# Row sums on the token partitions, inverses spread by a product, and another order of the attention's work

## The reference

```
q, k, v = norm(x) @ Wq, ctx @ Wk, ctx @ Wv      # x (4, 256, 128), ctx (4, 1601, 96)
attn = softmax(q k^T / 8)                       # per head, over 1601 keys
x = x + (attn v) @ Wo + bo
f = norm(x);  p = softmax(f @ router_w + router_b);  w = the two best of p
x = x + gelu(f @ sw1 + sb1) @ sw2 + sb2 + sum_e w_e (gelu(f @ rw1_e + rb1_e) @ rw2_e + rb2_e)
```

## Time and profile before

| | us |
|---|---|
| median of 3 runs (481.19 to 483.22) | 482.54 |
| the profiled execution | 480.71 |
| its span, first to last instruction | 478.9 |
| PE busy | 429.6 (90%) |
| DVE busy | 289.2 (60%) |
| POOL busy | 269.9 (56%) |
| ACT busy | 234.6 (49%) |

### The profile page before, as it was taken

One profiled execution on the slowest core, in us unless ns is written; L12 is line 12 of the kernel. 1 busy time (PEld: TensorE's weight loads), 2 busy tenths in 40 slices (PEclk: granted clock), 3 DMA queues, 4 the chain that ended last, 5 costly groups with the idle time before them and its releaser, 6 DMA issues. The chain is left out here.

```text
span 478.9 us, 9185 instructions
## 1 busy us (share of the span) xinstructions
PE 429.6 (90%) x3462; PEld 321.0 (67%) x3462; DVE 289.2 (60%) x595; ACT 234.6 (49%) x367; POOL 269.9 (56%) x184
## 2 busy tenths in 40 slices
PE   8999978988998986988998959898998896999997
PEld 7667655756674855665876738585857574687896
DVE  4666665766724764676627664767356773768653
ACT  5645370624381704351763516152826071579873
POOL 6209872958570747555721749091805479067982
PEclk9979988999999997999999997999999998999999
DMA  7400000200000002000000011000000000320500
GB/s 236 96 1 2 1 2 1 53 1 2 1 0 1 2 1 52 2 1 0 2 1 1 2 55 47 1 2 1 0 1 2 0 3 1 97 81 1 177 23 23
DMA packets 17138, 11.73 MB, mean 24 GB/s; under 512 B 10188, under 2 KB 14136, under 8 KB 17096
## 3 DMA queue, kind: packets, MB, share of 16 engines
q1 hardware_dynamic: 17096, 11.15, 8.8%
HBM read 10.55 MB, written 0.56 MB: 23 GB/s over the span
## 5 line engine op out<-in xcount | busy, mean ns | idle before, releaser
L908 DVE TENSOR_REDUCE maxes<-ps 128x1 f32<-128x402 f32 x256 | 133.1, 569 | 85.8 <-PE ps L1094 85.4
L792 ACT ACTIVATE probs<-ps 128x1024 f32<-128x1024 f32 (+1 forms) x112 | 104.0, 962 | 156.4 <-PE ps L1153 155.1
L489 POOL TENSOR_TENSOR work<-work,probs 128x1024 f32<-128x1024 f32 x60 | 142.7, 2378 | 4.8 <-POOL work L487 0.2
L1169 PE MATMUL ps<-probs,v_sb 128*64 128x256 f32 (+1 forms) x832 | 101.7, 391 | 0.0
L487 POOL TENSOR_TENSOR work<-probs 128x1024 f32<-128x1024 f32 x15 | 35.9, 2393 | 114.7 <-issue 93.6
L1169 PEld LDWEIGHTS ps<-probs,v_sb 128*64 128x64 f32 (+1 forms) x832 | 56.8, 139 | 33.4 <-issue 10.5
L905 DVE TENSOR_TENSOR kq_lo<-ps,kq_hi 128x402 fp32r<-128x402 f32 (+2 forms) x80 | 41.8, 544 | 55.0 <-ACT kq_hi L753 54.0
L1094 PE MATMUL ps<-kq_hi 64*128 64x402 f32 x256 | 60.0, 413 | 8.0 <-DVE maxes L908 7.1
L1153 PE MATMUL ps<-kq_hi,kq_lo 64*128 64x256 f32 (+1 forms) x416 | 62.1, 291 | 0.0
L1153 PE MATMUL ps<-kq_lo,kq_hi 64*128 64x256 f32 (+1 forms) x416 | 62.0, 291 | 0.0
L1153 PE MATMUL ps<-kq_hi 64*128 64x256 f32 (+1 forms) x416 | 62.0, 291 | 0.0
(11 more groups left out here) (149 smaller groups left out, 629.7 us busy)
## 6 DMA issues: line engine op xcount, KB each, us to landing
v_sb<-weight_rows SPq DMA_DIRECT2D x12, 256.0 KB, 3.8
raw<-in_ctx_T_dram SPq DMA_DIRECT2D x3, 600.4 KB, 4.6
work<-in_L_ffn_rw_dram SPq DMA_DIRECT2D x1, 1024.0 KB, 7.0
shift_rows<-neg_row SPq DMA_DIRECT2D x64, 0.5 KB, 2.0
raw<-weight_rows SPq DMA_DIRECT2D x4, 256.0 KB, 3.6
raw<-in_ctx_T_dram SPq DMA_DIRECT2D x3, 150.8 KB, 2.6
x_sb<-in_x_dram SPq DMA_DIRECT2D x1, 384.0 KB, 4.8
wo_sb<-in_L_xattn_Wo_dram SPq DMA_DIRECT2D x1, 256.0 KB, 6.5
```

Of the source, the lines that this page charges most:

```text
L489: ops.tensor_tensor(acc, acc, pr, ALU.add).then_inc(summed, 1)
L792: nc.scalar.activation(dst, src, ACT.Exp, scale=SCALE).then_inc(probs_ready, 1)
L908: v.tensor_reduce(maxes[:, p % 2, i * T + t, blk:blk + 1], src[:, 0:BW], AX.X, ALU.max).then_inc(ring_taken, 1)
L1169: ins = mm(o_bank[DH * i:DH * (i + 1), :], v_sb[0:rows, c, h * DH:(h + 1) * DH], probs[0:rows, n % SLOTS, i, j * S:(j + 1) * S], start=(c ...
```

## The change

- The folded sums are now the stationary operand and a single column of ones the moving one: four products of a result of 128 tokens by 1 (head i, token tile t) put the row sums on the token partitions, 4 columns in all. DVE takes the reciprocal of 128x4 numbers, once. This is the item "sums".
- A new item "spread": four products of a broadcast column of reciprocals with the identity give 64 equal rows for each head and tile, the inverses spread over 128 partitions as before. ACT copies the 128x256 result to SBUF (`inverse`), and DVE multiplies o_bank by it in one instruction of 128x256.
- All 16 maxima of pair n+1 stand beside the scores of pair n: a couple ahead of unit 0 and one behind each unit. None stands among the values.
- The sums of pair n-1 come behind the scores of pair n, the spread behind the first two projections. The add stands ahead of the values in the list, which on DVE is ahead of the next maxima as before.
- y and roots stand ahead of the context's splits, and norm stands behind the third unit of scores of the pair after. roots no longer waits for the add of its pair.
- DVE and not POOL folds the sums of pair 0 too; the statistics of x (stats) stand ahead of the scores of pair 0; normal one pair earlier; POOL's part of the w2 split (w2_low) behind the values of pair 14.

The diff, cut to its core:

```diff
-AMONG_VALUES = ((0, 2), (3, 4), (5, 2))
-BEHIND_VALUES = 2
...
     for n, (b, p) in enumerate(order):
-        ahead = maxima[n + 1][before_scores:] if n + 1 < n_order else []
-        behind = 2 if n == 1 else 0
+        ahead = maxima[n + 1] if n + 1 < n_order else []
+        out += ahead[:2]
         for u in range(n_units):
             out.append(("scores", (b, p, u)))
-            if n and u in (behind, behind + 2):
-                out.append(("quotient", order[n - 1] + ((u - behind) // 2,)))
...
+            out += ahead[2 * u + 2:2 * u + 4]
+            if u == 2 and p == 2 and b:
+                out.append(("norm", b - 1))
+        if ahead:
+            out.append(("shift", order[n + 1]))
...
+        if n:
+            out.append(("sums", order[n - 1]))
+            projections = projections[:2] + [("spread", order[n - 1])] + projections[2:]
...
+        if b and p == 1:
+            out += [("ring", ("y", b - 1)), ("roots", b - 1)]
...
+        out.append(("add", (b, p)))
+        out += [("values", (b, p, u, j)) for u, unit in enumerate(key_units(chunks)) for j in range(len(unit))]
+        if n == n_order - 2:
+            out += [("w2_low", e) for e in range(experts)]
...
-    amid = {0: [("sums", last_pair), ("quotient", last_pair + (0,)), ("quotient", last_pair + (1,))], 2: [("ring", ("y", b))], 5: [("ring", ("xt", b))],
+    amid = {0: [("sums", last_pair)], 1: [("spread", last_pair)], 2: [("ring", ("y", b))], 5: [("ring", ("xt", b))],
...
-            return "dve" if pair and u == NU - 1 or pair == B * PAIRS - 1 else "pool"
+            return "dve" if u == NU - 1 or pair == B * PAIRS - 1 else "pool"
...
                 if kind == "roots":
-                    if w + 1 < B:
-                        added(w + 1, 1)
                     inverse_roots(slice(w * T, w * T + T), B + w + 1)
...
+                elif kind == "spread":
+                    pair = w[0] * PAIRS + w[1]
+                    act.wait_ge(spread_filled, pair + 1)
+                    if pair:
+                        act.wait_ge(sums_taken, pair)
+                    nc.scalar.copy(inverse[:], sums_bank).then_inc(inverse_ready, 1)
...
-            def quotient(b, p, i):
-
-                pair, q = b * PAIRS + p, slice(i * P, i * P + P)
-                dve.wait_ge(sums_filled, pair + 1)
-                v.reciprocal(rden[:, q], sums_bank[:, q]).then_inc(rden_ready, 1)
-                dve.wait_ge(rden_ready, 2 * pair + i + 1)
+            def quotient(b, p):
+
+                pair = b * PAIRS + p
+                dve.wait_ge(inverse_ready, pair + 1)
...
-                v.tensor_tensor(oT[:, b % 2, p, q], o_bank[:, q], rden[:, q], ALU.mult).then_inc(sums_taken, 1)
+                v.tensor_tensor(oT[:, b % 2, p, :], o_bank, inverse[:], ALU.mult).then_inc(sums_taken, 1)
...
+                if kind == "sums":
+                    dve.wait_ge(sums_filled, w[0] * PAIRS + w[1] + 1)
+                    v.reciprocal(rden[:].rearrange("p h t -> p (h t)"), sums_bank[:, 0:2 * T]).then_inc(rden_ready, 1)
...
                 pe.wait_ge(summed, (pair + 1) * (NU - 1))
-                for i in range(2):
-                    ins = mm(sums_bank[DH * i:DH * (i + 1), :], ones[:, :],
-                             psum_keys[:, pair % 2, i, 0:S], start=True, stop=True)
+                for j in range(2 * T):
+                    i, t = divmod(j, T)
+                    ins = mm(sums_bank[:, j:j + 1], psum_keys[:, pair % 2, i, t * P:(t + 1) * P], ones[:, 0:1],
+                             start=True, stop=True)
                 ins.then_inc(sums_filled, 1)
+
+            def spread_inverses(b, p):
+
+                pe.wait_ge(rden_ready, b * PAIRS + p + 1)
+                for t in range(T):
+                    for i in range(2):
+                        ins = mm(sums_bank[DH * i:DH * (i + 1), t * P:(t + 1) * P],
+                                 rden[:, i, t:t + 1].to_broadcast([P, DH]), idr, start=True, stop=True)
+                ins.then_inc(spread_filled, 1)
```

More of the change, by code:

```diff
@@ L67, in plan @@
         out += pair_of_maxima + v0[3 + i:4 + i]
-    out.append(("shift", order[0]))
+    out += [("shift", order[0])] + [("stats", t) for t in range(1, batches)]
     rest = v0[len(couples) - 1:]
@@ L72, in plan @@
         out += [x] + rest[2 + i:3 + i]
-    out += rest[2 + len(second):] + maxima[1][:before_scores]
+    out += rest[2 + len(second):]
     for n, (b, p) in enumerate(order):
-        ahead = maxima[n + 1][before_scores:] if n + 1 < n_order else []
-        behind = 2 if n == 1 else 0
+        ahead = maxima[n + 1] if n + 1 < n_order else []
+        out += ahead[:2]
         for u in range(n_units):
             out.append(("scores", (b, p, u)))
-            if n and u in (behind, behind + 2):
-                out.append(("quotient", order[n - 1] + ((u - behind) // 2,)))
[L82 to L88, removed]
+            out += ahead[2 * u + 2:2 * u + 4]
[3 more added lines that the diff above has]
+            out.append(("shift", order[n + 1]))
         vs = [("ring", ("v", b, c)) for c in range(chunks)] if p == 0 and b else []
         projections = keys(n + 2)
+        if n:
+            out.append(("sums", order[n - 1]))
+            projections = projections[:2] + [("spread", order[n - 1])] + projections[2:]
         if vs:
@@ L98, in plan @@
         if n == 0:
-            out += [("stats", t) for t in range(1, batches)]
+            out += [("normal", t) for t in range(1, batches)]
         if n == 1:
-            out += [("normal", t) for t in range(1, batches)] + [("ring", ("xn", 0)), ("ring", ("xn", 1))]
+            out += [("ring", ("xn", 0)), ("ring", ("xn", 1))]
+        if b and p == 1:
+            out += [("ring", ("y", b - 1)), ("roots", b - 1)]
         if p == 1 and b + 1 < batches:
@@ L288, in build @@
         ones = sb("ones", [P, DH])
-        rden = sb("rden", [P, S])
+        rden = sb("rden", [P, 2, T])
+        inverse = sb("inverse", [P, S])
         oT = work[:, 1, :].rearrange("p (a b c) -> p a b c", a=2, b=PAIRS)
@@ L1048, in _ @@
                     row_sums(*w)
+                if kind == "spread":
+                    spread_inverses(*w)
                 if kind == "ring":
```

10 lines of the change are left out of this document (5 added, 5 removed).

## The result

The changed kernel takes 425.4 us (425.1 to 425.6), the kernel before 481.9 in the same series: a ratio of 0.8825, with a 95% interval from 0.8795 to 0.8854. The profiled execution took 425.6, its span 423.8 of it, at a mean granted clock of 0.992 (before 0.968).

What follows compares the result with a forecast made beforehand. The prediction took PE, busy nine tenths of the span, as the bound. Its terms, 9.3 + 9.0 + 25 + 16.4 - 2.8 - 0.9 = 56 us, took 480.7 to 424.7; forecast 425, range 417 to 430.

Steps and rivals of the forecast that it cites:

- A plain pair: Middle pairs: pitch falls from 21.1 to 18.6 us, 2.5 a pair, 25 over ten pairs.
- Maxima beside the scores: All maxima fit beside the scores, 8.3 us from first couple to scores' end; no waiting for DVE booked.
- the bound of two units: Scores: a loop of PE filling and ACT emptying, 2.35 us for two units; two couples of maxima just fit in.
- The rival of the maxima's queue: DVE's queue of maxima sets the scores' pace: 1.1 us per pair over 15 pairs, 441 us; chance 0.15.
- Sums and spread: New products on PE in each pair: sums 0.9 us, spread 0.75 with changes of tile.
- The thin cover for the reciprocal: Before the spread, PE's sums and projections cover DVE's reciprocal with 0.2 us to spare; 0.1 booked.
- The slower rival: Each of the sixteen small steps waits for its own weight load, 0.44 us each: 510 us; chance 0.02.
- Start and pair 1: Pair 1 begins at 43.75 instead of 53.04, 9.3 us gained; pair 1 itself gains 9.0.
- The terms of pair 0: Pair 0, without sums: 8.3 + 2.7 + 0.2 + 5.83 = 17.0 us.
- Pairs 6 and 10: Stall at the third unit and low clock behind it go, 0.7 booked for norm: 16.4 us gained together.
- Pairs 14 and 15: No projections cover the chain: 19.2 and 17.5 us, together 36.7 against 33.9, 2.8 lost.
- Experts: The experts' sums and spread cost 0.9 us more.

Runs made afterwards that it cites:

- e1: The changed kernel with ten of each pair's maxima back among and behind the values, six in the scores, DVE's add behind them: 460.4 us, ratio 0.9575.
- e3: The changed kernel with the old product of ones and 256-column reciprocal at the new place, no spread, no copy by ACT: 412.8 us, ratio 0.8592.
- e7: The changed kernel with every reduction of maxima over 201 of its 402 columns: 422.5 us, ratio 0.8783.
- e2: The changed kernel with the old sums back behind their own pair's values, DVE's reciprocals and products in the next scores: 424.6 us, ratio 0.8834.
- e6: The changed kernel with the four products of the sums done twice over, in one piece of sixteen steps: 468.2 us, ratio 0.9716.
- e4: The changed kernel with only the normalisation's places undone (inverse roots on POOL, normalisation on ACT): 428.4 us, ratio 0.8925.
- e9: The kernel before with only the normalisation's places changed, y moved with them: 471.7 us against 481.3, ratio 0.9807.
- e5: The changed kernel with pair 14's sums and spread moved behind the first and second units of pair 15's scores: 420.7 us, ratio 0.8727.
- e10: The changed kernel with the sums' products done twice, first behind the fourth unit of scores, then at the usual place: 438.4 us, ratio 0.9085.

## Why the prediction was right, and where its terms were off

- **A plain pair.** 18.65 for 18.6, and the ten pairs gained 26.0 for 25. The parts of the gain add up: 1.9 from the places of the maxima (e1), the wait of 1.02 for the add and the idle 0.52 for ACT gone, less 0.9 that the new method costs PE (e3), are 2.5. No run undoes the add's place alone, so its 1.02 is read from the rows.
- **Maxima beside the scores.** The forecast had them at no more than a couple in the bound of two units, and 2.54 + 1.02 a pair gone among the values. Measured: six units 6.97 for 7.1, values in one run, 1.9 a pair back in e1. The scores take 8.45 and not 8.3 because the last small unit with its couple takes 1.20 for 0.9. The rival of the maxima's queue had the right place and the wrong size: e7 shows 0.21 a pair, where the rival had 1.1 and the forecast nothing.
- **Sums and spread.** The sums took 0.92 for 0.9, the spread 0.58 by itself and about 0.8 with the change of tile on either side of it, for 0.75. The thin cover for the reciprocal held, since no plain pair waits in front of the spread. The forecast entered the method as a cost, and e3 shows that it is only that. What the place behind the next scores gains, 11.8 us by e2 and e3, the method spends again.
- **The slower rival** had each small step wait for its own load, 0.44. A step takes 0.115, with a load of 128 columns each. Small steps can cost more, but through the clock (e6), which no term held.
- **Start and pair 1.** Pair 1 begins at 44.12 for 43.75, and gains 9.1 for 9.0. (The terms of pair 0 come to 17.0, and the sum for its end used 17.2; measured 17.5.) For pair 1 the forecast named the normalisation of x, one pair earlier. No run moves that alone; e1, which keeps it, still loses 5.4 of the 9.1, so the maxima's places had a part in it.
- **Pairs 6 and 10.** They gained 16.9 for 16.4. Pair 6 is 0.7 longer than pair 7, for 1.0 booked (xt and norm). That the gain came from the places of roots and norm was half wrong: in the changed kernel they are worth 3.0 (e4), alone 9.6 (e9).
- **Pairs 14 and 15.** The terms mis-sized: 39.1 us for 36.7, and that from two errors. Pair 14 took 17.8 for 19.2, since its waits were 0.3 and 0.2 and not 0.7 and 1.1. Pair 15 took 21.35 for 17.5. Its five additions took 7.5 us on DVE (343.82 to 351.31) for the 6.3 of the forecast, so PE waited 2.41 + 1.02 for some 2, and the last values took 8.65 where the term had 5.83. A wait of 3.4 us costs its length and the low clock behind it, as the earlier trace rows had shown at another place; e5 takes both away.
- **Experts.** 0.6 more for 0.9.

Up to pair 14 the change gained 1.2 us more than the terms, in the last two pairs it lost 2.4 more. These errors stand against each other, and the span came to 423.8 for 423 because of that too: the mechanism of the plain pairs was right, the closeness of the total in part luck.

## What to carry to other kernels

Work out a change edit by edit, since one of them can be a cost that the others hide: here a cheaper reciprocal for DVE was paid with PE's time, while DVE had 2.7 us of projections and 5.8 of values as cover. An engine's place in the queue mattered more than its work: the same maxima at other places were worth 35 us. Where the last pass of a loop has none of the work that covers a chain in the others, start that chain earlier; here it was worth 5 us, and 8 with the wide reciprocal.

## What the runs showed of the hardware

Products of one column count as busy in the profile, and PE's clock fell behind a piece of sixteen of them (1.81 us, granted clock 0.56 over the 3.8 us behind it), where PE had not been idle at all; it did so behind ten of fourteen such pieces, and in e10 behind none of the pieces of eight in pairs 1 to 13. The Trainium skill, page "TensorE: Matmul & The Clock Gate", Part 1, says that the gate goes by "how busy the PE has been recently". If busy means the busy time of the profile, the trace does not agree: PE's was full before the fall. Which property of these steps counts (their width, or the loads between them) was not tried, nor why four pieces left the clock alone.

DVE's addition over 128x512 takes 0.69 in a plain pair, but in pair 14 of e5, as in the changed kernel, it took 1.20 while POOL split the experts' weights; whether POOL is the cause was not tried:

```profile
338.99 1.20 DVE L484 TENSOR_TENSOR work<-work 128x512 f32<-128x512 f32 x1 [1.06 <-POOL work L482]
```

A reciprocal of 256 columns took 1.75 us, two of 128 took 0.95 each, one of 4 columns 0.17.
